# Five hand-written orders of steps laid anew in an eight-sequence, two-layer kernel; zero-operand matmuls moved out of the scan stages

## The reference, cut to what matters

```python
x = layernorm(x + attention(x))      # 16 heads of 8; standard and "line" scores, two softmaxes, mixed by a gate
x = layernorm(x + ffn_fp4(x))        # blockwise 4-bit quantization of x and of the hidden 352, silu(gate) * up
x = layernorm(x + mamba(x))          # rms norm, conv of 4, silu, delta/B/C, a scan over 256 tokens for 256 x 16 states
x = layernorm(x + lowrank_ffn(x))    # W1, W2 plus products of 16 token rows of the same sequence, gelu between
```

## Time and profile before

| | us |
|---|---|
| median of 3 runs | 825.11 (821.05 to 826.53) |
| the profiled execution | 825.88 |
| its span, first to last instruction | 824.1 |
| mean granted TensorE clock | 0.915 |

### The profile page before, as it was taken

One profiled execution on the slowest core, in us unless ns is written; L12 is line 12 of the kernel. 1 busy time (PEld: TensorE's weight loads), 2 busy tenths in 40 slices (PEclk: granted clock), 3 DMA queues, 4 the chain that ended last, 5 costly groups with the idle time before them and its releaser, 6 DMA issues. The chain is left out here.

```text
span 824.1 us, 12171 instructions
## 1 busy us (share of the span) xinstructions
PE 712.8 (86%) x4422; PEld 423.6 (51%) x4422; DVE 619.5 (75%) x1083; ACT 409.3 (50%) x832; POOL 394.3 (48%) x475
## 2 busy tenths in 40 slices
PE   5468988997899888998899889997999889986867
PEld 2234545455645655555655655555655555554324
DVE  1277077998879866986989887988899778953692
ACT  1212633954397245843378248824682448433532
POOL 5543132694178413853269324962493018501671
PEclk9565999999999989996999999999999898967899
DMA  5321211431045101521054103520262114100410
GB/s 136 79 99 47 83 42 34 170 109 65 9 170 160 46 0 35 203 89 58 9 162 150 32 33 101 155 87 35 67 184 69 58 42 150 34 1 0 155 57 8
DMA packets 41241, 66.40 MB, mean 81 GB/s; under 512 B 8041, under 2 KB 30398, under 8 KB 38846
## 3 DMA queue, kind: packets, MB, share of 16 engines
q1 hardware_dynamic: 39006, 64.58, 24.4%
q10 hardware_dynamic: 2176, 1.05, 0.4%
HBM read 57.68 MB, written 7.86 MB: 80 GB/s over the span
## 5 line engine op out<-in xcount | busy, mean ns | idle before, releaser
L586 POOL TENSOR_TENSOR shared<-u,bcrow 128x512 f32<-128x512 f32 x128 | 203.6, 1620 | 64.1 <-DMA bcrow<-bc_dram 34.3
L963 DVE TENSOR_TENSOR_SCAN shared<-ps_f,shared 128x512 f32<-128x512 f32 x128 | 151.1, 1208 | 11.8 <-ACT ps_f L733 7.1
L865 DVE TENSOR_REDUCE mx<-ps_s 128x2 f32<-128x512 f32 (+1 forms) x192 | 126.0, 686 | 38.5 <-PE ps_s L1005 34.3
L1005 PE MATMUL ps_s<-stack_mem 72*128 72x128 bf16 (+3 forms) x1024 | 143.7, 260 | 7.7 <-DVE mx L865 5.6
L1005 PE MATMUL ps_y<-shared,ident 128*128 128x512 f32 (+1 forms) x288 | 121.8, 553 | 8.8 <-DVE shared L972 8.0
L733 ACT ACTIVATE ps_f<-delta,amat 128x255 f32<-128x255 f32 x256 | 109.8, 475 | 28.3 <-DVE shared L963 28.2
L1005 PE MATMUL ps_y<-zero_bf 128*128 128x512 bf16 x419 | 119.5, 409 | 1.9 <-DVE zero_bf L806 1.1
L1005 PEld LDWEIGHTS ps_s<-stack_mem 74*128 74x128 bf16 (+1 forms) x1024 | 83.8, 102 | 63.0 <-DVE mx L865 19.4
L670 ACT ACTIVATE probs<-ps_s 128x512 f32<-128x512 f32 x192 | 104.7, 595 | 22.7 <-PE ps_s L1005 22.1
L551 POOL TENSOR_TENSOR rstd<-mv,cst 128x2 f32<-128x2 f32 x32 | 6.2, 195 | 185.3 <-DVE mv L786 185.3
L972 DVE TENSOR_TENSOR shared<-shared,bcrow 128x1024 f32<-128x1024 f32 x56 | 78.9, 1409 | 1.8
(11 more groups left out here) (213 smaller groups left out, 1063.4 us busy)
## 6 DMA issues: line engine op xcount, KB each, us to landing
bcrow<-bc_dram SPq DMA_DIRECT2D x64, 512.0 KB, 4.2
stack_mem<-stack_dram SPq DMA_DIRECT2D x96, 192.0 KB
stack_dram<-parts SPq DMA_DIRECT2D x24, 256.0 KB, 4.5
x_tm<-in_L_attn_x_dram ACTq DMA_DIRECT2D x8, 128.0 KB, 2.1
xb<-in_L_attn_x_dram SPq DMA_DIRECT2D x8, 128.0 KB, 2.2
out_dram<-y_out SPq DMA_DIRECT2D x8, 128.0 KB, 4.8
fmem<-in_L_attn_conv_w_dram SPq DMA_DIRECT2D x1, 512.0 KB
lmem<-in_L_ffn_W_dram SPq DMA_DIRECT2D x2, 256.0 KB
```

What stands on the lines that cost most here:

```text
L586: G.tensor_tensor(bx[:, j % 2, c], u[:, c].unsqueeze(1).to_broadcast([P, 2, T]), bcrow[:, j % RING, 0], ALU.mult).then_inc(bx_sb, 1)
L865: V.tensor_reduce(mx[:, a, min(i, 1), hd[0]:hd[-1] + 1:2], ps_s[:, n % 2].rearrange("p (h n) -> p h n", h=len(hd)), AX.X, ALU.max).then_in ...
L963: V.tensor_tensor_scan(hs[:, j % HB, c].rearrange("p n t -> p (n t)"), ps_f[:, c, :], bx[:, j % 2, c].rearrange("p n t -> p (n t)"), 0.0, ...
L1005: return nc.tensor.matmul(o, lhsT, rhs, start=start, stop=stop, **kw)
```

## The change

All five strings are written anew. No step's code changes, each stream has as many steps as before, and PE has 203 letters `w` in both. Two lines of PE's string stand for the rest, which is of the same kind:

```diff
@@ ORDER["pe"] @@
...
-        cccccwwcwwcccwwccccccccccsswwccccccNsswccccssccccsnssncpncpoppwwcclpcplffclfflwwwplwclcfccfccwwcc
...
+        mcccmcccccccccccccccccsccccsccccsccccNsccccscssnpwwnpnwppsspccwowwffpclcwcclfflwwlccwwlplfccwfww
...
```

More of the change, by code:

```diff
@@ L40 @@
     "sp": """
[L41 to L42 removed]
+        ppppppccpccpcppppcccrrprcpcrrpprrrrpplcccrrcrpprrcpprrrrppllcrcpcrprcrrppcrrrrppllcccrrpcrprrpcp
+        rrrrppllcrccrprpccrrpprrrrppllcrpcrrcrrpcppcrrrrppllcccrrrrrccrrrrllrrrrrrrrrlll
     """,
     "pool": """
[L45 removed]
@@ L51 @@
[L51 to L55, removed]
+        ppppppppppppppxpcxpxpccccpccccccccccccccccccccccpnpppppfpfpfcmmmmpmmccccscccsccsccsscsccccsscccs
@@ L56 @@
+        sccssccccsssscnpppppclfppflfpmmpmmmmcccssccccsccccscsccsccsscccsccssscsscccsscnppppplfcppflpfmmm
+        mpmmccsccscccsccccsscsccccsscccsssscccsscccsscpnppppflfcpplpfmmmmpmmccccsscccccssccscsccccsssccc
+        ssscccssccccsspnppppplpfflpfmcpmmmmmccccscccsccssccscsccccsscccsssccscsscccsscnppppplcppfflfpmmm
+        mpmmccccscccssccccscsccssccssscccssccscscccsscnlfcflfmmmmmmccccsscccsccscccsccsccsscccsssscccssc
+        ccsscnffllfmmmmmmssssssssssssssssll
     """,
     "dve": """
-        ppxpxxxxxxxxccccccccccpccccccccccccccccNnnccnfcfcfffppccfffffccccfccfcmcccccccmccccccmmsssssssss
@@ L64 @@
-        sssssssssNsssnssnonofoffffllffffflfflmmmmsssssssssssssssssssssssssooollll
+        ppxxpxxxxxxpccccccccccccccccccccccccccNnccnncffcfffpccccpfffffccfccfmcccccccmcccccccmmssssssssss
+        sssssssssssNsnsssccnoocncfocfcfffpccllpfffffxcclccfcfcmcccccmcccccccmmssssssssssssssssssssNssnss
+        slnocnoccfccfcofffpccpllfffffcclfccfcmcccccclmcccccccmmssssssssssssssssssssssNnnsssnfoffffoccocc
+        ccplplfffffcclfccfccmcccccccmcccccccmmssssssssssssssssssssNssnlsssnocconfoccffffplpcclccffffflcc
@@ L74 @@
[L74 to L77, removed]
+        pppppppxppppppxxccwwccccwccccccwcccccccpccccccccccccccccccccccccccccwccccccwcNccccnpccnnpcpwwpcp
+        pccwwffccffwwwwwwwwwwwpwfccfwccwcccmmmccmccmccmmccwccccccccccccccccccsccwwccccsccsccccsNccccswww
@@ new lines @@
+        wcsnsnpccnpsspopccpwwclcccplfflffcclwwwwwwlpwwlfcwcfwcccwwwwwwwmccmmmccmccmccmccwccccccccccccccc
+        cccccccssccccccssNccccscsnswnnsspccowccpcpcpccwwpwplwflfwwlfflwwwlcpclfwwwfccwwwwwcccmcmmcmccmcc
+        mcccmcccccccccccccccccsccccsccccsccccNsccccscssnpwwnpnwppsspccwwowffpclcwcclfflwwlccwwlplfccwfww
+        ccwwwwwwccmcmmccmccmccmccmccwwcccwcccccccccccccsccccsccccsccccwsNccccscspnsnpnsspccowpccppwwwlwl
+        ccfflccffwwlwwwwcplcwlfwfwccwwwcccmwmmccmccmccmwccmccwccccccccccccccccsccccsccccccccNssccccsscnp
@@ L78 @@
+        snnccwsspoppccwwplcclwwwccwpwwfflfflpwwwccwwlwwlfwfwccwcccwmcmcmmccmccmccmccwccccccccccccccccccc
+        cccssccwNsccsccscccccssnssnnccowwwwwccwclwcwflflccfflwwlwwcclfccfwcccwwwwwwmccmmccmccmccmmwccccc
+        cccccccccccccwccccccsNsccsccccssccccscsnnnsswwwwwwoffffllwwwwllwwwwlwwwfwwflwwwmmmmwmmwmsswsswws
+        swwwsssowwwwwlwwwwlllllwwwwwww
     """,
```

21 lines of the change are left out of this document (6 added, 15 removed).

## The result

The changed kernel takes 813.9 us in the median (813.2 to 814.6, four runs) against 825.6 of the kernel before beside it (821.1 to 826.5): a ratio of 0.9869, 95% interval 0.9831 to 0.9907. The sign and the range were right. Of the 27 us forecast 12 came. The profiled execution took 814.0, its span 812.3.

A forecast was written before the change was run, and what follows sets the result against it. Bounds: DVE's scan chain, PE in two scan stages, and middle-stretch chains through PE, ACT and DVE hanging on PE's clock. 825.9 us less 8.8, 16.4, 5.5, 1.0, 2.0, 2.0, plus 1.0 and 7.6, gave 799; range 784 to 823.

The forecast's parts named there:

- Term 5: First six middle stretches: 53 extra zero steps, a third of them in the way, cost 7.6 us (bounds 0 to 22.8).
- Term 7: SP, ACT, POOL and the rest of DVE: steps changing places cost nothing, with bounds of 4 us either way.
- Term 1: Scan stages: fewer zero steps bring the four later ones to 31.2 us, 8.8 less; 1.0 shifts to a middle stretch.
- Term 2: The two 62.5 us middle stretches: more zero steps hold the clock, each falls to 54.3, 16.4 us less.
- Term 3: Last middle stretch: gate and up products ahead of the low-rank ffn, more zero steps, 5.5 us less (bounds 0 to 9).
- Term 4: The middle stretch from 631.1, clock 0.90, 51.6 us: 1 us less (bounds 3 less to 3 more).
- Term 6: Start and end: setup step ahead of the scores, zero matmuls moved from the last products; 2 us less at each.
- rival A: Clock still falls in some middle stretches, so half the gain of terms 2 and 3 comes: 810 us; chance 0.17.
- Rival B: Zero steps do not change the clock; scan stages, start and end still gain: about 820 us; chance 0.15.
- Rival C: PE's queue between gate and down products: zero steps stand in the way, clock stays low: 848 us; chance 0.09.
- Rival D: Clock now falls in the scan stages, where fewer zero products stand: 849 us; chance 0.03.

The follow-up runs named there:

- the second run: Changed kernel with one letter of POOL's order moved and DVE's two attention-end steps put behind the last three scan steps of the 38.5 us stage: 815.6 us.

## Why the prediction was right in its sign and wrong in its size

The step that failed is the cost of the new middle stretches beside their clock. Term 5 took a third of the moved zero steps to be in the way, on the ground that PE's idle time of 43 us has room for the rest; with one product more in each step, a half to two thirds of it lengthened the stage. Term 7 took the new order of the other engines' steps to cost nothing; in the fifth stretch it put 2.6 us of DVE's own work ahead of xq and 1.9 us of waiting ahead of the scores. And stretches 1 and 4, taken to keep their full clock, lost it (0.89 and 0.94).

By the cuts the spans differ by 11.9 us. Against the forecast:

- *Term 1, scan stages, 8.8 less.* The four later ones lost 6.9 (133.5 to 126.6): right, PE's queue was the bound, and 34.9 became 30.4. But the three earlier ones, taken to stay as they were, grew by 2.5, 0.9 and 7.3. Of the 7.3, 6.3 went over from the next middle stretch, as the second run shows; this leaves 4.4. The forecast had allowed 1.0 for such a shift, behind the stage of 34.9 us.
- *Term 2, the two long stretches, 16.4 less.* 17.0 came by the cuts (56.0 and 52.0), and would pass for a hit. With the 6.3 us that moved over taken out, 10.7 remain. The target, the mean of three stretches, was too low: by the letters those held 10, 13 and 4 zero steps and the long ones now hold 18 and 17, and these cost time at full clock too. By the trace's cuts the first of the two had 34 zero products before and has 36 now, so its 6.5 us came from their places and the order, not from their number.
- *Term 3, the last stretch, 5.5 less.* 8.3 came. It is the order that does it, given some filler: 46.7 us in the new order with the old places, 58.1 in the old order with the new ones, and 53.7 in the new order without any. The forecast had named the order, gate and up products ahead of the low-rank ones.
- *Term 4.* One less was forecast, 1.9 more came, though the clock rose from 0.90 to 1.00.
- *Term 5, zero steps in the way, 7.6 more.* "A third of them in the way" was a choice without a row. By 0.136 us a product, 0.27 a step, 53 steps cost 14.4 us. By the trace's cuts the six stretches hold 85 products more, and at 0.10 to 0.15 us that is 8 to 13. Both are estimates from the runs with three products. The three stretches that had their clock grew from 56.7, 53.6 and 52.6 to 60.4, 57.3 and 57.0, 11.8 more in sum, but two of them lost clock as well, and only the third is a price at full clock.
- *Term 6, start and end, 4 less.* 1.6 and 2.4 came.
- *Term 7, the other engines, nothing.* POOL's preparation was free, as said. DVE's steps were not: two of them moved 6.3 us from a stretch to a scan stage, which is nothing in sum, but in the fifth stretch DVE's order and the scores' place cost time that no zero product explains.

Terms 2, 4 and 5 together were to give 9.8 us and cost 3.0 with the 6.3 us taken out; that is 12.8 of the 15.2 us missed. The price of a step explains between nothing and 7 of them. The rest is the clock that still fell in stretches 1 and 4 (rival A's mechanism, right in part) and the new order itself; how it divides between these two is not shown. Without zero steps the middle stretches 1 to 6 take 368.1 us in the new order and 360.3 in the old one, but the first is read from an execution 6.4 us above its median, and as whole kernels the two lie 2.4 us apart. That the measured time fell within the range is in part luck, as terms 3 and 5 missed on opposite sides.

Rival B is excluded: the same order without zero steps in the middle lost 35 us and its clock. By the rule of the Trainium skill that the prediction weighed (page "TensorE: Matmul & The Clock Gate", section "HAM oscillation — how this bites in real kernels") it is long pauses between bursts that lose the clock. These traces agree in part: in the first stretch the clock fell behind a pause of 3.26 us, but at 573.1 none was above 1.30. Rival C named the right mechanism, steps in the way, for a clock that stays low; in the old order the new places cost some 15 us though the clock of the two long stretches rose. Rival D did not come: the scan stages kept 1.00 but for one, at 0.97, and the last, at 0.86, which took its 28.7 us all the same, as DVE bounds it.

Still open: why the clock falls in one kernel and stays in another behind the same instructions, why stretch 4 loses it with no pause above 1.20 us ahead of the fall at 470.0, and what makes a place good. No rule of place held in both orders. In stretch 1 a zero step in PE's wait for x3 was not tried. How much the new order of the real steps gains by itself, with zero steps fitted to it but nothing else, is not separable from these runs.

## What to carry to other kernels

Before filler is moved or added in a fixed queue, measure what it costs there by itself, by making each piece a little larger at unchanged places in a stretch whose clock is full already; here that was a half to two thirds of the piece's own time, and all of it where PE was the bound. A stretch that holds its clock with few pieces should get no more. Compare a stage only together with its neighbour where steps cross the cut, or a shift passes for a gain.
